# Reading each chunk's block number from its index list instead of from a transfer of its own, in the cosine pass of a four-layer graph network

## The reference

```python
h = jnp.maximum(_layernorm(x, axis=-1), 0.0)
x = x + _L0_gnn_ref(h, src, dst, 12500)
...
Hn = H / jnp.maximum(norm, EPS)
scores = jnp.sum(Hn[row] * Hn[col], axis=1)
m = jax.ops.segment_max(scores, row, num_segments=num_nodes)
e = jnp.exp(scores - m[row])
s = jax.ops.segment_sum(e, row, num_segments=num_nodes)
attn = e / s[row]
out = jax.ops.segment_sum(attn[:, None] * H[col], row, num_segments=num_nodes)
```

## Time and profile before

| | |
|---|---|
| median of 3 runs | 12968.3 us (12966.79 to 12970.97) |
| the profiled execution's own time | 12962.94 us |
| its span in the profile | 12961.2 us |
| busy: POOL, VectorE, TensorE, ScalarE | 66%, 48%, 16%, 12% |
| the cosine pass, first to last gather | 1684.0 to 3891.1 us of the span |

### The profile page before, as it was taken

How to read it: one execution, slowest core, us unless ns; L and a number is a source line. 1 busy time by engine, 2 the same in 40 slices (tenths; PEclk the granted TensorE clock), 3 DMA queues, 4 the chain that set the end, 5 groups by cost and what they waited for, 6 DMA issues and landing times. The chain is left out here.

```text
span 12961.2 us, 105933 instructions
## 1 busy us (share of the span) xinstructions
PE 2048.0 (16%) x7272; PEld 1358.7 (10%) x7272; DVE 6250.2 (48%) x20840; ACT 1599.7 (12%) x5546; POOL 8526.3 (66%) x8805
## 2 busy tenths in 40 slices
PE   8830000000001000000000000002111123333334
PEld 6630000000001000000000000001000012222223
DVE  9992333333344454545444444313222237777765
ACT  0000000000001000000000000001000014444443
POOL 0007467677775777777677777677777757777775
PEclk9855555555555555555555555555555555555555
DMA  0001223333321222222111211113222224444442
GB/s 11 0 14 39 25 27 27 26 28 28 27 27 22 32 35 34 33 35 34 26 29 28 30 29 29 25 26 75 51 51 51 51 71 107 107 108 107 107 101 63
DMA packets 1006515, 575.48 MB, mean 44 GB/s; under 512 B 757826, under 2 KB 855635, under 8 KB 1005953
## 3 DMA queue, kind: packets, MB, share of 16 engines
q0 software_dynamic: 307520, 409.04, 19.5%
q1 hardware_dynamic: 587723, 101.69, 4.8%
q10 hardware_dynamic: 111088, 63.12, 1.6%
HBM read 485.71 MB, written 87.37 MB: 44 GB/s over the span
## 5 line engine op out<-in xcount | busy, mean ns | idle before, releaser
L981 POOL DMA_INDIRECT got<-gat_tab,list x3280 | 3124.1, 952 | 1157.2 <-issue 971.1
L981 POOL DMA_INDIRECT got<-rel_tab,list x1640 | 1642.2, 1001 | 655.1 <-issue 451.9
L981 POOL DMA_INDIRECT got<-h_tab,list x1640 | 1569.7, 957 | 674.6 <-issue 487.3
L981 POOL DMA_INDIRECT got<-gcn_tab,list x1640 | 1561.6, 952 | 574.4 <-issue 492.0
L1764 DVE TENSOR_REDUCE chunk_sum<-got 128x64 f32<-128x256 f32 (+1 forms) x436 | 239.7, 550 | 1443.6 <-DMA got<-gcn_tab,list 1305.9
L1067 DVE TENSOR_TENSOR prod<-got,h 128x256 f32<-128x256 f32 (+1 forms) x436 | 180.2, 413 | 1308.4 <-DMA got<-h_tab,list 1203.0
L543 POOL DMA_INDIRECT info_tab<-info,rank_i x98 | 125.4, 1279 | 976.7 <-DVEq L520 947.1
L2285 PE MATMUL p_gate<-got,ident 128*128 128x256 f32 (+1 forms) x872 | 510.4, 689 | 1382.4 <-DVE gate L2122 1377.2
L1453 DVE COPY e<-top 128x4 f32 (+1 forms) x872 | 185.4, 213 | 1111.5 <-DMA got<-gat_tab,list 860.4
L1698 PE MATMUL p_t<-ident,hg 128*128 128x128 f32 x98 | 24.6, 429 | 3978.7 <-DVEq L1576 2014.2
L1629 ACT ACTIVATE p<-e 128x20 f32<-128x20 f32 (+3 forms) x872 | 185.4, 213 | 3651.5 <-DVE e L1472 3494.9
(11 more groups left out here) (433 smaller groups left out, 8085.3 us busy)
## 6 DMA issues: line engine op xcount, KB each, us to landing
own<-own_tab SPq DMA_DIRECT2D x436, 160.5 KB, 2.4
got<-gat_tab,list POOLq DMA_INDIRECT x3280
rel_tab<-rows ACTq DMA_DIRECT2D x98, 386.0 KB, 2.8
got<-h_tab,list POOLq DMA_INDIRECT x1640
got<-gcn_tab,list POOLq DMA_INDIRECT x1640
got<-rel_tab,list POOLq DMA_INDIRECT x1640
own_tab<-own ACTq DMA_DIRECT2D x98, 160.5 KB, 3.3
chunks_src<-rows_src SPq DMA_DIRECT2D x480, 4.5 KB
```

The source lines that it names most:

```text
L981: pool.indirect_dma_start(r.got[:, q, j, :], None, table, at(r.lists[s][:, c, j:j + 1]))\
```

## The change

The lists of the cosine pass become 9 columns wide, so that a list transfer brings the whole row of each chunk and node, the block number with it. The transfer `meta` is not issued in this pass, neither is the wait ahead of it. VectorE reads the block numbers out of the lists, from partition 0: `listed_blocks` takes the place of `turn_blocks`. It waits for list 0, loads two numbers with a load each, waits for list 1 and loads the other two. The lists are released where they were.

```diff
-def load_lists(nc, sp, lists, part, r, i, tab, columns):
+def load_lists(nc, sp, lists, part, r, i, tab, columns, blocks_apart=True):
...
             .then_inc(r.list_in[s], 16)
+    if not blocks_apart:
+        return
     sp.wait_ge(r.meta_used, i + 1)
...
+def listed_blocks(nc, eng, engines, r, i, last):
+
+    b = []
+    for s in range(STAGES):
+        eng.wait_ge(r.list_in[s], i * 16 + 16)
+        eng.sem_inc(r.tick, 1)
+        for c in range(PER_STAGE):
+            b.append(eng.value_load(r.lists[s][0:1, c, last:last + 1], min_val=0, max_val=BLOCKS - 1))
+    return b
...
-        r = ring_buffers(m, part, CW)
+        r = ring_buffers(m, part, CW, columns=CROW)
...
-                    load_lists(nc, sp, lists, part, r, i, lists.chunk_tab, part.slots)
+                    load_lists(nc, sp, lists, part, r, i, lists.chunk_tab, r.columns, False)
...
-                b = turn_blocks(nc, dve, DVE, r, i)
+                b = listed_blocks(nc, dve, DVE, r, i, CROW - 1)
```

## The result

The changed kernel takes 12932.2 us in the median of 10 runs (12920.7 to 12936.0), the kernel before 12967.8 beside it (12958.6 to 12973.4). The ratio is 0.9971, with a 95% interval from 0.9961 to 0.9980: 26 to 51 us faster, 35.6 between the medians. The forecast was 28 us faster, 12940 on the scale of the runs shown before.

The account below looks back on a forecast made before the run. The prediction took a two-turn loop between SP and POOL to bound the cosine pass's first part. Terms -35 + 0 + 7 = -28 us gave 12940 us from 12968.3, with an 8-in-10 range of 12924 to 12960.

Parts of the forecast that it names:

- What bounds part one: Cosine pass: SP's lap (list 1 to next list 0, 20.9 us), landings and POOL's gathers sum to 45.5 us over two turns.
- The full lap counts: Rival, part one: each wait shrinks by all that SP saves, gain 64 us, 12904 us; chance 0.06.
- SP loses 1.0 us: Part one: without the block numbers' transfer SP's time from list 1 to next list 0 falls 1.0 us; gain 35 us.
- The upper bound: SP's saving per turn at most 1.2 us, if the register load behind the transfer shortens too; gain 42 us.
- The lower bound: SP's saving at least half of 1.0 us, if the next transfer takes over issue time as back-pressure; gain 17 us.
- Gains nothing in the other turns: Part one outside the 71 turns, as 42 to 61 near POOL's own 20.0 us: SP's saving is worth nothing.
- Wider lists cost nothing: Lists growing from 16 to 36 bytes a row: cost 0, bounds 0 to 0.2 us of later landing, 8 us.
- VectorE's reads: Four loads instead of one, 1.1 us at each turn's head: 0 in part one, 7 us in part two, bounds 0 to 11.
- Mostly given back: Rival: any two of half the issue time moving on, reads costing 11 us, later landing; gain 2 to 18 us; chance 0.25.
- Slower: Rival: 36-byte pieces land later; 0.7 us later uses up the gain, 1.3 us makes it 26 us slower; chance 0.04.
- The sum: Whole kernel: -35 from SP, 0 from wider lists, +7 from part two's reads, -28 us.
- The likeliest case: Whole kernel: a gain of 18 to 38 us, 12930 to 12950 us; chance 0.61.

## Why the prediction was right, point by point

- **What bounds part one**: a loop over two turns between SP and POOL, so that the lap counts half. Right, and shown three ways: the lap fell by 1.2 us and the turn by 0.49 to 0.56; it grew by 0.62 to 0.85 and the turn by 0.30 to 0.44; with the wait taken out of the lap and no work with it, 104 us went.
- **The full lap counts** (rival): refuted by the same runs.
- **SP loses 1.0 us.** Undersized: 1.22 in the rows above. The upper bound named the reason, the register load behind, at least 0.458 us before and 0.27 after. The lower bound, half of the issue time taken over by the next transfer, falls: the five writes behind took 4.39 us before and 4.36 after. Why the issue of so small a transfer is long, and why a load right behind it is slow, no run tells.
- **Gains nothing in the other turns.** Wrong by 3.8 us: in turns 42 to 61, with a lap of 15.7 us in those of six writes, the loop still came to 20.1 a turn, and they fell from 20.45 to 20.25. The first stretch in turn gave 20.2 where half of 1.2 in 41 turns would be 25. Its turns of six writes, now 20.4 us, come near POOL's 20.0 and gave 0.4 each; but the kernel changed in part one alone gave (2608.67 - 1704.01) - (2581.41 - 1704.65) = 27.9 there, so one profile can't say that this stretch fell short. SP writes the table of the later passes in turns 42 to 89 and its last two blocks behind the lists of turn 95. That last lap was to gain a whole microsecond and gained none: it took 27.24 us and takes 27.30. With the third stretch, and 1 us lost at the ends, part one gained 39.8, where the sum had 35.
- **Wider lists cost nothing.** Right: the kernel with them alone stands at 1.0001. In the changed kernel, where POOL waits for list 0 behind a turn of ten writes, it starts 2.6 to 3.4 us after that list's issue, 2.85 in the middle value; before it was 2.6 to 3.6, and 2.78.
- **VectorE's reads: nothing in part one, 7 us in part two.** Right in part two and nearly so in part one. There the cover of 3.43 us is often gone: of the 95 first products from turn 1 on, 54 now wait for VectorE's own queue and no longer for a gather, 29 before. It cost little all the same, 2.7 us in the light turns and nothing in the others by the kernel that still issues the transfer. Part two lost 6.3, and gave it back when it read as before. In part two's timeline after, the last chunk's product, then the next turn's first, then that of chunk 1, then POOL:

```profile
3795.91 0.29 DVE L1080 TENSOR_TENSOR prod<-got,h 128x128 f32<-128x128 f32 x1 [0.90 <-DMA got<-h_tab,list]
...
3802.08 0.29 DVE L1080 TENSOR_TENSOR prod<-got,h 128x128 f32<-128x128 f32 x1 [3.57 <-issue]
...
3802.95 0.29 DVE L1080 TENSOR_TENSOR prod<-got,h 128x128 f32<-128x128 f32 x1
...
3805.83 0.94 POOL L983 DMA_INDIRECT got<-h_tab,list  x1 [1.27 <-DMA list<-chunks_src]
```

  VectorE's own queue now holds it up for 3.57 us, 2.52 in the earlier trace rows, and in every second turn POOL waits, here 1.27 us, for the list that is released late, where its idle time was the step of 0.30.

  The Trainium skill's floor of about 600 ns for such a load ("DMA: Bandwidth & Descriptors", section "Latency and other measured facts") is not what these runs show: 305 ns, and with 600, by the prediction's estimate from that page, part two would have lost 12.
- **Mostly given back** (rival): it needed two of three bounds. Half of the lap and later landing are refuted by the profile and by the wide lists alone, and the third, 11 us in part two, came to 6.
- **Slower** (rival): it rested on lists that land later, which the wide lists alone refute.
- **The sum**: -28 forecast, -33.5 in the pass (-39.8 and +6.3), -35.6 between the medians. The likeliest case stands; the terms that were too small are SP's lap and the light turns. That it came this close has some luck in it: half of the lap's measured 1.2 us in 71 turns would be 43, the two stretches gave 37 in this profile, and the light turns, put at nothing, made up 4 of the difference.

What stays open: the 7 us that the profiled last pass took longer are within what that pass does in other profiles, and were not followed further. Nor were the 11 us between two part ones of the same instructions, which make every attribution of a few microseconds to one stretch uncertain.

## What to carry to other kernels

Where two engines wait for each other a turn apart, a saving inside the loop counts once in the whole loop, as it did here for SP: divide it by the number of turns that the loop spans, and look for the wait inside the lap, since taking that out was worth three times what taking work out was. A transfer of sixteen bytes on a busy issuing queue cost its issue here, with the step around it 1.0 us, and 0.2 more in the load behind it. Data that ride along in another transfer have to be read where they lie: four numbers side by side took one load, the same four in two buffers took three and a half times as long.

## What the runs showed that I had not expected

A register load of VectorE took 305 ns for one number, 343 ns for four that lie side by side, and 516 ns for two that lie 36 bytes apart. And SP's register load right behind the transfer of the block numbers took 458 to 506 ns, against 263 to 285 behind a list.
